# Two batches rounded together in the last feed-forward layer, and layer 1 attention's output product moved into the next batch's first gap

## Chip, cores and metric

One NeuronCore of a Trainium2 chip runs the whole kernel. The metric is the device time of one execution in microseconds (us), the median of three. PE is TensorE (its matrix engine), PEld its weight loads, DVE is VectorE, ACT is ScalarE, POOL is GpSimd, SP is SyncE, which issues the DMAs. Matmul results land in eight PSUM banks, called `banks` in the profile; all else lies in SBUF, in one large tensor called `memory`.

## What is computed

A four-layer decoder on x of shape 8 batches x 112 rows x 256 columns, float32; each layer is attention, cross attention and a feed-forward part, each behind a layer norm and added to x. Two of the twelve parts matter here.

Layer 1 attention (16 heads of 16), with a fixed near-diagonal matrix L mixed into the attention:

```
A_stable = LAMBDA_JUMP * A + (1.0 - LAMBDA_JUMP) * L[None, None, :, :]
out = jnp.einsum('bhqk,bhkd->bhqd', A_stable, V)
out = out.transpose(0, 2, 1, 3).reshape(B, S, D)
return out @ Wo.T + bo
```

The last part, layer 3's feed-forward, rounds the inputs of all three matmuls to four-bit values with a scale for each block of 16:

```
amax = jnp.max(jnp.abs(xb), axis=-1, keepdims=True)
sc = jnp.clip(amax / FP4_MAX * global_scale, 0.0, FP8_MAX)
sc8 = sc.astype(jnp.float8_e4m3fn).astype(jnp.float32)
dq = sc8 / global_scale
a = jnp.clip(jnp.abs(xb) / safe_dq, 0.0, FP4_MAX)
q = jnp.sign(xb) * _FP4_VALS[jnp.digitize(a, _FP4_MIDS)]
...
gate_out = nvfp4_linear(x, gate_w, s_in[0])
up_out = nvfp4_linear(x, up_w, s_in[0])
hidden = jax.nn.silu(gate_out) * up_out
return nvfp4_linear(hidden, down_w, s_in_down[0])
```

The hidden rows are 8 x 112 x 1024.

## The kernel before

The twelve parts run one after the other, with a barrier of all engines between them. Within a part every engine has its own program, written by walking one generator, `order()`, which yields steps such as ("turn", 3); each engine emits what it has to do for a step and skips the others. Nothing reorders afterwards: an engine works its own list strictly in this order and waits on semaphores (`wait_ge`) for the others. So `order()` sets what stands behind what on each engine.

**Layer 3's feed-forward, class `L3Ffn`.** It quantizes ten units of 112 x 1024: units 0 and 1 are the normalized input rows ("rows", four batches side by side), units 2 to 9 the hidden rows of batches 0 to 7. For a unit, DVE takes each block's largest magnitude (`tensor_reduce`), works out the scales in nine small instructions on 64 columns (`four_bit_scales`), scales the unit (`tensor_tensor`), clamps it and cuts out each value's power of two (two `tensor_scalar`), multiplies that to a rounding constant (a third `tensor_scalar`), and adds and subtracts the constant (two `tensor_tensor`): that rounds. GpSimd multiplies by the block scales and writes bf16 (`four_bit_values`). PE transposes the unit (step "turn"), ACT copies it out of PSUM; for hidden units PE then multiplies by the down weights and DVE adds the result to x (step "sum"). Step "gate" is the gate and up matmuls of a batch (PE), the Silu (ACT), and their product into `hids` (DVE, the "hid" instruction). In `order()` a hidden unit b is rounded ("four", b + 2), then comes gate b + 1, then the sum of b - 1, then the turn of b.

**Layer 1 attention, class `L1Attn`** on `TiledSelf`. For batch b: the scores of all 16 heads ("all", PE), their maxima (four `tensor_reduce` on DVE), 16 exponentials (ACT, "weights"), four groups of transposes ("turned"), a transposed table of 1/sum ("inverse"), the products with V ("products"), their scaling on DVE ("norm", into `oT`) and the addition of the near-diagonal part on GpSimd, then the output product ("y", PE). The projections k, q, v, the near-diagonal product and the norm of coming batches fill gaps between these; the tuple `plan` says which step of which batch (0, +1, +2) stands in which of five gaps: after turned 0, 1, 2, behind turned 3 and the exponentials, and at the batch's end. PSUM banks for y, k, q, near, v, xT, inverse and products are handed out in turn from a ring of two (6 and 7) by `next_bank`; `fill` makes PE wait until the bank's last content has been read. So whichever step stands two places further back in PE's list must have been read before a step may start.

## Time and profile before

| what | value |
|---|---|
| median of 3 runs | 2310.19 us (2309.71 to 2314.41) |
| the profiled execution's own time | 2309.87 us |
| its span | 2308.1 us |
| busy PE / DVE / ACT / POOL over the span | 88% / 59% / 39% / 24% |
| TensorE clock granted, mean | 0.865 of full speed |
| layer 1 attention in the trace | 640.29 to 748.83 us |
| layer 3's feed-forward in the trace | 2185.85 to 2303.25 us |

In a timeline row stand: start in us, length in us, engine, line, operation, out<-in with partitions x elements, how many were merged (x8), and in brackets how long the engine sat idle before it and who ended that. In a windows row stand: stretch, its length, then busy us (and count of instructions) of PE, PEld, DVE, ACT and POOL, then the granted TensorE clock (1.00 is 2.4 GHz, half of it 1.2 GHz), the DMA share and GB/s. In a group row stand: count | busy us, mean ns of one | idle before. Consecutive instructions of one engine that do not depend on each other overlap by about 0.1 us at their ends.

### The profile page before, as it was taken

The page shows a single profiled execution, that of the slowest core. Times are in us where ns is not written, and L with a number is a line of the kernel's source. Part 1 is how long each engine was busy: PE and PEld are TensorE (multiplying, and loading weights), DVE is VectorE, ACT ScalarE, POOL GpSimd, SP SyncE. Part 2 cuts the span into 40 slices and gives each one's busy share as a digit, 9 for nine tenths or more (in the row PEclk, how much of TensorE's full clock was granted, in tenths as well). Part 3 has the DMA queues.
Part 4 walks back from the last instruction along what each step waited for, and adds up shares of the span by engine and source line. Part 5 has one row for each costly group of instructions (what it writes and reads, how often), then busy time and mean ns, then how long its engine had stood idle before and what let it go on. Part 6 is the DMA issues. An engine that isn't in the chain of part 4 may idle for free.

```text
span 2308.1 us, 57670 instructions
## 1 busy us (share of the span) xinstructions
PE 2019.8 (88%) x22720; PEld 1471.6 (64%) x22720; DVE 1353.8 (59%) x3602; ACT 896.5 (39%) x3421; POOL 561.4 (24%) x1358
## 2 busy tenths in 40 slices
PE   8999999989977898998977887999999999789744
PEld 4899998877566565567855654666554545556522
DVE  6667666755255787545635624787263220678797
ACT  2455554543155564212334422665110111256511
POOL 3566664222011000102425512331000000401111
PEclk9555555999989899899988988999999999889956
DMA  3000002004000001100030000000030000000000
GB/s 136 4 5 5 5 5 79 1 1 182 0 5 2 14 12 53 86 0 24 1 133 2 1 1 7 9 11 2 1 151 0 1 0 4 1 15 12 2 0 16
DMA packets 8027, 57.21 MB, mean 25 GB/s; under 512 B 793, under 2 KB 5249, under 8 KB 5985
## 3 DMA queue, kind: packets, MB, share of 16 engines
q1 hardware_dynamic: 7760, 53.54, 6.1%
q8 instruction: 183, 3.00, 0.5%
q14 instruction: 84, 0.68, 0.1%
HBM read 52.62 MB, written 0.92 MB: 23 GB/s over the span
## 4 chain that ended last, share of the span: by engine, by line
PE 67%; DVE 12%; issue 9%; ACT 6%; POOL 5%; DMA 1%; POOLq 0%; DVEq 0%; SPq 0%; ACTq 0%
PE banks L265 43%; PE banks L270 8%; PE banks L1364 7%; PE banks L937 3%; ACT memory L985 2%; PE banks L963 2%; DVE memory L1466 2%; PE banks L1517 1%; DVE memory L1247 1%; ACT memory L1391 1%; DVE memory L824 1%; POOL memory L1423 1%; ACT memory L1398 1%; DVE memory L1472 1%; DVE memory L1475 1%
## 5 line engine op out<-in xcount | busy, mean ns | idle before, releaser
L265 PE MATMUL banks<-memory 128*112 128x256 f32 (+7 forms) x4192 | 1129.8, 425 | 65.9 <-POOL memory L2077 8.0
L265 PEld LDWEIGHTS banks<-memory 128*128 128x128 f32 (+3 forms) x4192 | 704.8, 195 | 396.4 <-issue 250.9
L270 PE MATMUL banks<-memory 112*125 112x112 f32 (+3 forms) x2000 | 305.9, 286 | 108.6 <-DVE memory L824 54.9
L270 PEld LDWEIGHTS banks<-memory 112*125 112x125 f32 (+3 forms) x2000 | 238.6, 172 | 224.6 <-issue 114.6
L1364 PE MATMUL banks<-memory 128*128 128x8 bf16 (+2 forms) x10752 | 308.1, 174 | 13.7 <-DVE memory L1449 1.4
L1364 PEld LDWEIGHTS banks<-memory 128*128 128x128 bf16 x10752 | 296.7, 104 | 25.7 <-POOL memory L1423 21.5
L985 ACT ACTIVATE memory<-banks,memory 112x375 f32<-112x375 f32 x384 | 215.4, 579 | 25.5 <-DVE memory L1023 25.1
L1023 DVE TENSOR_REDUCE memory<-banks 112x2 f32<-112x750 f32 x192 | 171.1, 934 | 37.1 <-PE banks L937 36.9
L1466 DVE TENSOR_REDUCE memory<-banks 128x48 f32<-128x192 f32 x448 | 122.1, 291 | 62.6 <-PE banks L1364 47.9
L840 POOL TENSOR_TENSOR memory<-memory 112x1 f32<-112x1 f32 x71 | 39.2, 552 | 355.7 <-DVE memory L819 354.3
L1031 DVE COPY memory<-banks 125x448 f32<-125x448 f32 x192 | 117.0, 620 | 10.5 <-PE banks L270 6.1
L1545 ACT ACTIVATE memory<-memory 112x112 f32<-112x112 f32 x192 | 71.7, 375 | 87.8 <-DVE memory L1566 87.8
L937 PE MATMUL banks<-memory 32*112 32x375 f32 x768 | 88.5, 529 | 19.5 <-ACT memory L985 17.3
L1007 ACT COPY memory<-banks 125x448 f32<-125x448 f32 x96 | 51.2, 533 | 127.8 <-PE banks L270 127.8
L3213 DVE TENSOR_TENSOR memory<-banks,memory 112x256 f32<-112x256 f32 x8 | 3.4, 425 | 157.6 <-PE banks L265 157.6
L1391 ACT ACTIVATE memory<-memory 128x48 f32<-128x48 f32 x224 | 54.4, 243 | 97.5 <-DVE memory L1466 97.4
L1405 ACT COPY banks<-memory 128x48 f32<-128x48 f32 x448 | 80.1, 179 | 23.8 <-DVE memory L1445 23.8
L1230 ACT ACTIVATE memory<-banks,memory 112x112 f32<-112x112 f32 x256 | 86.4, 391 | 6.7 <-DVE memory L1247 5.3
L3187 ACT ACTIVATE memory<-banks,memory 128x448 f32<-128x448 f32 x32 | 20.3, 635 | 173.5 <-PE banks L265 173.5
L985 ACT ACTIVATION_READ_ACCUMULATOR memory<-banks,memory 112x1 f32 x384 | 80.5, 210 | 0.0
L963 PE MATMUL banks<-memory 125*32 125x112 f32 x2304 | 76.2, 265 | 1.4 <-DVE memory L1031 1.4
L1423 POOL TENSOR_TENSOR memory<-memory 128x16 f32<-128x16 f32 x224 | 49.9, 223 | 102.2 <-ACT memory L1398 102.1
(234 smaller groups left out, 2425.2 us busy)
## 6 DMA issues: line engine op xcount, KB each, us to landing
memory<-in_l2x SPq DMA_DIRECT2D x1, 7680.0 KB, 21.6
memory<-in_l2f SPq DMA_DIRECT2D x1, 7168.0 KB, 20.1
memory<-in_l1f SPq DMA_DIRECT2D x1, 4617.0 KB, 14.8
memory<-in_ctxT SPq DMA_DIRECT2D x24, 187.5 KB
memory<-in_l2f SPq DMA_DIRECT2D x1, 4096.0 KB, 12.6
memory<-in_l3f SPq DMA_DIRECT2D x1, 3073.0 KB, 22.4
memory<-in_l2a SPq DMA_DIRECT2D x1, 3072.0 KB, 18.2
memory<-in_l0f SPq DMA_DIRECT2D x1, 2304.0 KB, 9.1
```

Of the source, the lines that this page charges most:

```text
L265: ins = self.nc.tensor.matmul(out, weights[i], acts[i], start=i == 0, stop=i == n - 1)
L270: return self.nc.tensor.transpose(out, in_, self.ident[0:n, 0:n])
L937: ins = PE.matmul(k.bank(bank, S, CK), q, kT, start=True, stop=True)
L963: ins = PE.matmul(k.banks[32 * r:32 * r + 32, 6, t * S:(t + 1) * S], v, PT_sb[0:CR, c, r * S:(r + 1) * S], start=c == 0 and m == 0, stop=c ...
L985: self.nc.scalar.activation(self.P_both[gi % 2][:, r, :], self.k.bank(r, S, CK), ACT.Exp, bias=u["nmax"][:, 4 * i + r:4 * i + r + 1], scal ...
L1023: V.tensor_reduce(u["nmax"][:, 4 * i + 2 * h:4 * i + 2 * h + 2], k.banks[0:S, 2 * h:2 * h + 2, 0:CK], AX, ALU.max, negate=True).then_inc(* ...
L1031: V.tensor_copy(self.PT_both[gi % 2][0:CR, c, :], k.bank(k.at["turn", gi, c], CR, 4 * S)).then_inc(*s.pt_v.up())
L1230: A.activation(self.P_all[:, i, g, :], k.bank(i, S, 4 * S)[:, g * S:(g + 1) * S], ACT.Exp, bias=u["nmax"][:, 4 * i + g:4 * i + g + 1], sca ...
L1364: ins = self.nc.tensor.matmul(own[:, part:3, at:at + B], self.whh[:, part, l, j, g * P:(g + 1) * P], self.upper[l][:, 0:3 - part, j * B:(j ...
L1391: A.activation(self.gates[:, l, 1:4, :].rearrange("p g c -> p (g c)"), self.sums[:, l, 0:6 * B], ACT.Tanh).then_inc(*s.act_tanh.up())
L1405: self.nc.scalar.copy(self.slots[l][last][:, 3, :], src).then_inc(*self.s.xw_in.up())
L1466: V.tensor_reduce(self.sums[:, l, first * B:end * B], self.slots[l][last].rearrange("p s c -> p c s"), AX, ALU.add).then_inc(*s.gates_in.up())
```

## The change

In layer 1 attention y of batch b moves from gap 4 of batch b to gap 0 of batch b + 1 (the last one behind the loop), stats moves two gaps earlier, xn one gap earlier, and v from gap 2 into gap 3, where xT joins it. In layer 3's feed-forward hidden units are rounded two at a time: the small scale instructions work on 128 columns and the scaling on 2048; the constant's multiplication goes from DVE to ACT as `Relu(ROUND * t - ROUND)`, and the two `tensor_tensor` become two `scalar_tensor_tensor` that put ROUND back. GpSimd starts both products of a pair when the second difference is done; the last two units' products go to DVE. The transposes alternate between two banks, `hT` has two buffers, and the walk of `order()` is written anew.

```diff
 class L1Attn(TiledSelf):
...
-    plan = ((("k", 0, 1),), (("q", 0, 1), ("near", 0, 0)), (("v", 0, 1), ("stats", 0, 2)), (("xn", 0, 2),),
-            (("xT", 0, 2), ("y", 0, 0)))
-    tail = ()
+    plan = ((("y", 0, -1), ("k", 0, 1), ("stats", 0, 2)), (("q", 0, 1), ("near", 0, 0)), (("xn", 0, 2),),
+            (("v", 0, 1), ("xT", 0, 2)), ())
+    tail = (("y", 0),)
...
+ROUND = 1.5 * 2.0 ** 22
...
 class L3Ffn:
...
     def order(self):
         yield "norm", B - 1
-        yield "four", 0
-        yield "four", 1
+        yield "rows", 0
+        yield "powers", 0
+        yield "round", 0
         yield "turn", 0
+        yield "rows", 1
+        yield "powers", 1
         yield "gate", 0
-        yield "turn", 1
-        for b in range(B):
-            yield "four", b + 2
-            if b + 1 < B:
-                yield "gate", b + 1
-            if b:
-                yield "sum", b - 1
+        yield "hid", 0
+        yield "gate", 1
+        yield "round", 1
+        yield "top", 0
+        yield "hid", 1
+        yield "top", 1
+        for p in range(HALF):
+            last = p == HALF - 1
+            yield "scale", p
+            if not last:
+                yield "gate", 2 * p + 2
+                yield "hid", 2 * p + 2
+            if p:
+                yield "turn", 2 * p
+            yield "powers", 2 * p + 2
+            yield "powers", 2 * p + 3
+            if not last:
+                yield "gate", 2 * p + 3
+            yield "turn", 2 * p + 1
+            sums = [("sum", b) for b in (2 * p - 2, 2 * p - 1) if p]
+            if last:
+                yield from sums
+            yield "round", 2 * p + 2
+            yield "round", 2 * p + 3
+            if not last:
+                yield "hid", 2 * p + 3
+                yield "top", 2 * p + 2
+                yield "top", 2 * p + 3
+                yield from sums
+        for b in (B - 2, B - 1):
             yield "turn", b + 2
-        yield "sum", B - 1
+        for b in (B - 2, B - 1):
+            yield "sum", b
...
+    def dve_round(self, n):
+        k, s, V = self.k, self.s, self.nc.vector
+        y, t = self.half(self.y, n), self.half(self.t, n)
+        V.wait_ge(*s.step_ready(n + 1))
+        V.scalar_tensor_tensor(out=y, in0=t, scalar=ROUND, in1=y, op0=ALU.add, op1=ALU.add).then_inc(*s.vstep.up())
+        V.wait_ge(*s.vstep.now())
+        V.scalar_tensor_tensor(out=y, in0=t, scalar=ROUND, in1=y, op0=ALU.add,
+                               op1=ALU.subtract).then_inc(*s.sums_ready.up())
+        if n >= self.LAST - 1:
+            V.wait_ge(*s.sums_ready(n + 1))
+            V.wait_ge(*s.tp16_full(n - 1))
+            four_bit_values(V, self.values[n % 2], y, self.scales(n)[:, 1]).then_inc(*s.last_ready.up())
...
     def pool(self):
+        norm_row(k, B - 1, k.stats, s.stat_ready(1), s.rstd_ready).then_inc(*s.xn_ready.up())
+        for n in range(self.LAST - 1):
+            G.wait_ge(*s.sums_ready(n + 1 if n < 2 else (n | 1) + 1))
+            if n >= 2:
+                G.wait_ge(*s.tp16_full(n - 1))
+            four_bit_values(G, self.values[n % 2], self.half(self.y, n), self.scales(n)[:, 1]).then_inc(*s.quant_ready.up())
...
     def act(self):
         k, s, A = self.k, self.s, self.nc.scalar
+        A.wait_ge(*s.wq_ready(1))
+        A.activation(self.sg[:, 0:1], self.minus, ACT.Silu)
         for step, i in self.order():
-            if step == "gate":
+            if step == "powers":
+                t = self.half(self.t, i)
+                A.wait_ge(*s.pow_ready(i + 1))
+                A.activation(t, t, ACT.Relu, bias=self.minus, scale=ROUND).then_inc(*s.step_ready.up())
+            elif step == "gate":
```

Lines of shared helpers lie three further down in the changed kernel. These rows stand in DVE's list of the last part before, from one unit's reciprocal to the next unit's maxima (L3429 is the hid instruction, L3448 the sum):

```order
L2812 RECIPROCAL memory<-memory 112x64
L2800 TENSOR_SCALAR memory<-memory 112x64
L2794 TENSOR_TENSOR memory<-memory 112x1024
L2800 TENSOR_SCALAR memory<-memory 112x1024
L2798 TENSOR_SCALAR memory<-memory 112x1024
L2800 TENSOR_SCALAR memory<-memory 112x1024
L2794 TENSOR_TENSOR memory<-memory 112x1024
L3445 TENSOR_TENSOR memory<-memory 112x1024
L3429 SCALAR_TENSOR_TENSOR memory<-banks,memory 112x1024
L3448 SCALAR_TENSOR_TENSOR memory<-banks,memory 112x256
L3257 TENSOR_REDUCE memory<-memory 112x64
```

And these in the changed kernel, from one pair's reciprocal on (L3496 is the hid instruction, L3523 and L3525 the two of `dve_round`):

```order
L2815 RECIPROCAL memory<-memory 112x128
L2803 TENSOR_SCALAR memory<-memory 112x128
L2797 TENSOR_TENSOR memory<-memory 112x2048
L3496 SCALAR_TENSOR_TENSOR memory<-banks,memory 112x1024
L2803 TENSOR_SCALAR memory<-memory 112x1024
L2801 TENSOR_SCALAR memory<-memory 112x1024
L2803 TENSOR_SCALAR memory<-memory 112x1024
L2801 TENSOR_SCALAR memory<-memory 112x1024
L3523 SCALAR_TENSOR_TENSOR memory<-memory 112x1024
L3525 SCALAR_TENSOR_TENSOR memory<-memory 112x1024
L3523 SCALAR_TENSOR_TENSOR memory<-memory 112x1024
L3525 SCALAR_TENSOR_TENSOR memory<-memory 112x1024
```

Between scaling and difference, one unit's three `tensor_scalar` have become two units' two each; the two adds are of the fused form and stand in a block of four.

On ACT the last rows of the program before are these (L3505 is the Silu, L3516 the copy of a transposed hidden unit):

```order
L3505 ACTIVATE memory<-banks,memory 112x1024
L3516 COPY memory<-banks 128x896
L3505 ACTIVATE memory<-banks,memory 112x1024
L3516 COPY memory<-banks 128x896 x2
```

In the changed kernel they are these (L3585 is the Relu, L3590 the Silu, L3601 the copy):

```order
L3585 ACTIVATE memory<-memory 112x1024 x2
L3590 ACTIVATE memory<-banks,memory 112x1024
L3601 COPY memory<-banks 128x896 x2
L3585 ACTIVATE memory<-memory 112x1024 x2
L3601 COPY memory<-banks 128x896 x3
```

The last two Relus, of units 8 and 9, stand behind the copies of units 5 and 6 and ahead of those of units 7, 8 and 9.

In PE's list of layer 1 attention, with the semaphores that a row waits for, this stood before from turned 3 of a batch to turned 0 of the next (L265 with 112x256 is y, L1214 the products, L270 with 128x112 first the inverse and then xT):

```order
L270 MATMUL banks<-memory 112x112 [waits pt_a,exp_done]
L270 MATMUL banks<-memory 112x112 x3
L270 MATMUL banks<-memory 128x112 [waits near_ready,inv_ready]
L270 MATMUL banks<-memory 128x112
L1214 MATMUL banks<-memory 32x112 [waits pt_v,pt_a,v_ready]
L1214 MATMUL banks<-memory 32x112 x15
L270 MATMUL banks<-memory 128x112 [waits r_ready,xn_ready]
L270 MATMUL banks<-memory 128x112
L265 MATMUL banks<-memory 112x256 [waits o_ready,oT_ready]
L265 MATMUL banks<-memory 112x256
L270 MATMUL banks<-memory 112x112 [waits pt_a,exp_done]
```

And this stands there now, from behind turned 3 to y (the first L268 is v, the second y; L273 with 128x112 is first xT and then the inverse):

```order
L268 MATMUL banks<-memory 112x256 [waits q_ready,xT_ready]
L268 MATMUL banks<-memory 112x256
L273 MATMUL banks<-memory 128x112 [waits near_ready,xn_ready]
L273 MATMUL banks<-memory 128x112
L273 MATMUL banks<-memory 128x112 [waits v_ready,inv_ready]
L273 MATMUL banks<-memory 128x112
L1217 MATMUL banks<-memory 32x112 [waits pt_v,pt_a,xT_ready,v_ready]
L1217 MATMUL banks<-memory 32x112 x15
L273 MATMUL banks<-memory 112x112 [waits pt_a,exp_done]
L273 MATMUL banks<-memory 112x112 x3
L268 MATMUL banks<-memory 112x256 [waits r_ready,oT_ready]
L268 MATMUL banks<-memory 112x256
```

The inverse now waits for v_ready, because its bank held v, and the products for xT_ready.

## Rows read from the trace of the kernel before

**Rows 1.** Windows: six batches of layer 1 attention, one of them, the last part.

```profile
663.74:740.07 76.33, 61.62 (x694) 51.80 (x694) 41.99 (x120) 47.06 (x226) 8.84 (x17) 0.89 0.01 2
716.13:727.68 11.55, 9.04 (x117) 7.52 (x117) 7.21 (x21) 7.93 (x39) 1.56 (x3) 1.00 0.01 1
2185.85:2303.25 117.40, 49.50 (x208) 32.10 (x208) 106.50 (x181) 19.26 (x19) 21.11 (x12) 0.60 0.00 0
```

**Rows 2.** Timeline of DVE, one hidden unit of the last part.

```profile
2241.88 1.21 DVE L3257 TENSOR_REDUCE memory<-memory 112x64 f32<-112x1024 f32 x1
2243.12 0.25 DVE L2800 TENSOR_SCALAR memory<-memory 112x64 f32<-112x64 f32 x1
...
2245.73 1.23 DVE L2794 TENSOR_TENSOR memory<-memory 112x1024 f32<-112x1024 f32 x1
2246.99 0.69 DVE L2800 TENSOR_SCALAR memory<-memory 112x1024 f32<-112x1024 f32 x1
...
2249.18 1.23 DVE L2794 TENSOR_TENSOR memory<-memory 112x1024 f32<-112x1024 f32 x1
...
2251.58 1.28 DVE L3429 SCALAR_TENSOR_TENSOR memory<-banks,memory 112x1024 f32<-112x1024 f32 x1
...
2253.16 1.21 DVE L3257 TENSOR_REDUCE memory<-memory 112x64 f32<-112x1024 f32 x1
```

**Rows 3.** Timeline of DVE, a 128-column scale chain in the weights' quantization.

```profile
1715.13 0.29 DVE L2800 TENSOR_SCALAR memory<-memory 128x128 f32<-128x128 f32 x1
...
1718.47 2.29 DVE L2794 TENSOR_TENSOR memory<-memory 128x2048 f32<-128x2048 f32 x1
```

**Rows 4.** Groups by line and shape, of DVE and of ACT.

```profile
L2803 DVE SCALAR_TENSOR_TENSOR memory<-memory 112x256 f32<-112x256 f32 x1 | 0.4, 424 | 0.0
L1376 ACT ACTIVATE memory<-memory 128x1024 f32<-128x1024 f32 x2 | 2.1, 1050 | 0.0
```

**Rows 5.** Timeline of all engines, the first products and gates of the last part.

```profile
2196.81 1.93 POOL L3248 TENSOR_TENSOR memory<-memory 112x1024 bf16<-112x1024 f32 x1 [7.95 <-DVE memory L3445]
2197.89 0.90 DVE L2800 TENSOR_SCALAR memory<-memory 112x64 f32<-112x64 f32 x1
...
2204.65 1.11 ACT L3505 ACTIVATE memory<-banks,memory 112x1024 f32<-112x1024 f32 x1 [2.45 <-PE banks L265]
...
2206.99 1.28 DVE L3429 SCALAR_TENSOR_TENSOR memory<-banks,memory 112x1024 f32<-112x1024 f32 x1
...
2209.86 3.23 PE L265 MATMUL banks<-memory 128*112 128x512 bf16 x8
```

**Rows 6.** Timeline of all engines, the end of the last part.

```profile
2298.86 0.93 PE L3494 MATMUL banks<-memory 112*128 112x112 bf16 x8 [7.44 <-POOL memory L3248]
2299.82 0.91 ACT L3516 COPY memory<-banks 128x896 bf16<-128x896 bf16 x1 [10.41 <-PE banks L3494]
...
2302.77 0.48 DVE L3448 SCALAR_TENSOR_TENSOR memory<-banks,memory 112x256 f32<-112x256 f32 x1 [5.59 <-PE banks L265]
```

**Rows 7.** Timelines of PE and DVE in layer 1 attention: y, all, v's bias, maxima, last products.

```profile
716.13 1.12 PE L265 MATMUL banks<-memory 128*112 128x256 f32 x4 [0.82 <-POOL memory L2077]
717.08 0.55 PE L270 MATMUL banks<-memory 112*112 112x112 f32 x4
...
720.92 1.03 PE L265 MATMUL banks<-memory 128*112 128x256 f32 x4
...
735.08 1.05 PE L1190 MATMUL banks<-memory 32*112 32x112 f32 x32
...
735.19 0.49 DVE L1109 TENSOR_TENSOR memory<-banks,memory 112x128 f32<-112x128 f32 x2 [1.33 <-PE banks L265]
...
736.20 2.22 DVE L1247 TENSOR_REDUCE memory<-banks 112x4 f32<-112x448 f32 x4 [0.15 <-PE banks L1190]
...
744.51 0.98 PE L1214 MATMUL banks<-memory 112*32 112x112 f32 x32 [0.46 <-ACT memory L1238]
746.80 1.12 PE L265 MATMUL banks<-memory 128*112 128x256 f32 x4 [1.30 <-POOL memory L2077]
```

More of the change, by code:

```diff
@@ L3258, in four_bit_scales, with four_bit_steps @@
                     apply_absolute_value=True).then_inc(*s.vstep.up())
+def four_bit_scales(k, src, gs, sc, sign=1.0):
+    four_bit_tops(k, src, sc[:, 0])
+    four_bit_steps(k, gs, sc, sign)
+def four_bit_steps(k, gs, sc, sign=1.0):
+    c = Chain(k)
+    top, s8, c8 = sc[:, 0], sc[:, 1], sc[:, 2]
     c.ts(top, top, 1.0 / 6.0, gs, ALU.mult, ALU.mult)
@@ L3373 @@
     UNITS = (("rows", 0), ("rows", 1)) + tuple(("hidden", b) for b in range(B))
+    LAST = B + 1
     def __init__(self, k):
@@ L3380, in __init__ @@
         self.ident16 = take(P, dt=BF16)
-        self.y, self.t = [take(HID, parts=S) for _ in range(2)], take(HID, parts=S)
-        self.sc = [take(3, HID // 16, parts=S) for _ in range(2)]
+        two = lambda *dims, dt=F32: [take(*dims, dt=dt, parts=S) for _ in range(2)]
+        self.hids, self.y, self.t = two(2 * HID), two(2 * HID), two(2 * HID)
+        self.sc = two(3, 2 * HID // 16)
         self.xT = four_bit_rows(k)
-        self.values = [take(HID, dt=BF16, parts=S) for _ in range(2)]
@@ L3385, in __init__ @@
-        self.sg, self.hids = take(HID, parts=S), take(2, HID, parts=S)
-        self.hT = take(8, S, dt=BF16)
+        self.values = two(HID, dt=BF16)
+        self.sg = take(HID, parts=S)
+        self.hT = [take(8, S, dt=BF16) for _ in range(2)]
+        self.minus = take(1, parts=S)
     def order(self):
         yield "norm", B - 1
-        yield "four", 0
-        yield "four", 1
+        yield "rows", 0
+        yield "powers", 0
+        yield "round", 0
         yield "turn", 0
+        yield "rows", 1
@@ L3412, in run, with half, scales @@
+        for b in (B - 2, B - 1):
+            yield "turn", b + 2
+        for b in (B - 2, B - 1):
+            yield "sum", b
+    def half(self, a, n):
+        pair = a[(n // 2 + 1) % 2]
+        return pair[:, n % 2 * self.HID:(n % 2 + 1) * self.HID]
+    def scales(self, n):
+        return self.sc[(n // 2 + 1) % 2][:, :, n % 2 * self.HID // 16:(n % 2 + 1) * self.HID // 16]
     def run(self):
@@ L3421, in dve @@
     def dve(self):
-        k, s, V, st = self.k, self.s, self.nc.vector, self.k.stats
+        k, s, V, st, w = self.k, self.s, self.nc.vector, self.k.stats, self.w
+        V.memset(self.minus, -ROUND)
         V.tensor_copy(self.ident16, k.ident).then_inc(*s.wq_ready.up())
@@ L3426, in dve @@
                 norm_row_stats(k, i, st, s.stat_ready)
-            elif step == "gate":
+            elif step == "rows":
+                if i:
+                    V.wait_ge(*s.xn_ready(1))
+                src = k.row_norms[:, i * HALF:(i + 1) * HALF, :].rearrange("p b d -> p (b d)")
+                y = self.half(self.y, i)
+                four_bit_scales(k, src, w["s_in"][0:S, 0:1], self.scales(i), -1.0)
+                four_bit_scaled(k, src, y, self.scales(i))
+            elif step == "hid":
+                hid = self.half(self.hids, i + 2)
@@ L3428, in dve @@
                 V.wait_ge(*s.silu_ready(i + 1))
                 V.scalar_tensor_tensor(
-                    out=self.hids[:, i % 2, :].rearrange("p (h n) -> p h n", h=2), in0=k.banks[0:S, 2:4, :],
-                    scalar=self.inv[0:S, 1:2], in1=self.sg.rearrange("p (h n) -> p h n", h=2), op0=ALU.mult,
+                    out=hid.rearrange("p (h n) -> p h n", h=2), in0=k.banks[0:S, 2:4, :], scalar=self.inv[0:S, 1:2],
+                    in1=self.sg.rearrange("p (h n) -> p h n", h=2), op0=ALU.mult,
@@ L3432, in dve @@
                     op1=ALU.mult).then_inc(*s.hid_ready.up())
-            elif step == "four":
-                kind, b = self.UNITS[i]
-                if kind == "hidden":
-                    V.wait_ge(*s.hid_ready(b + 1))
-                elif b:
-                    V.wait_ge(*s.xn_ready(1))
-                if i >= 2:
-                    V.wait_ge(*s.quant_ready(i - 1))
-                src, gs = self.rows_of(i)
-                four_bit_scales(k, src, gs, self.sc[i % 2])
-                four_bit_sums(k, src, self.y[i % 2], self.t, self.sc[i % 2])
-                V.wait_ge(*s.vstep.now())
-                V.tensor_tensor(self.y[i % 2], self.y[i % 2], self.t, ALU.subtract).then_inc(*s.sums_ready.up())
+            elif step == "top":
+                V.wait_ge(*s.hid_ready(i + 1))
+                four_bit_tops(k, self.half(self.hids, i + 2), self.scales(i + 2)[:, 0])
+            elif step == "scale":
+                sc = self.sc[i % 2]
+                if i:
+                    V.wait_ge(*s.quant_ready(2 * i))
+                four_bit_steps(k, w["s_in"][0:S, 1:2], sc, -1.0)
+                four_bit_scaled(k, self.hids[i % 2], self.y[i % 2], sc)
+            elif step == "powers":
+                four_bit_powers(k, self.half(self.y, i), self.half(self.t, i), s.pow_ready)
+            elif step == "round":
+                self.dve_round(i)
```

66 lines of the change are left out of this document (29 added, 37 removed).

## The prediction

> **What bounds the kernel now.** I read the windows first, then each engine's timeline inside the two parts that the change touches, since a mean over the span mixes stages with different limits.
>
> In the last part DVE is busy 106.50 of 117.40 us, PE 49.50, ACT 19.26 and GpSimd 21.11 [rows 1]. Its list is the path: one hidden unit takes from one maxima instruction to the next 2253.16 - 2241.88 = 11.28 us, and none of the rows between shows an idle bracket [rows 2]. What the reader is to see there: the scale chain of nine small instructions takes 2245.73 - 2243.12 = 2.61, the scaling 1.26, each of the three passes over 1024 columns 2.19 / 3 = 0.73, add and subtract together 2.40, the hid instruction with the sum behind it 1.58, the maxima 1.24. PE, ACT and GpSimd only matter at the part's two ends.
>
> In layer 1 attention PE is the path. A batch takes 11.55 us at a granted clock of 1.00, with 9.04 us of PE work in it; the six batches from 663.74 on take 76.33 at 0.89 [rows 1]. So 76.33 - 6 x 11.55 = 7.0 us there go with the lower of the two clocks. PE's idle 11.55 - 9.04 = 2.5 us of a batch lie behind turned 3, in three pieces: ahead of the inverse, ahead of xT, and 0.82 ahead of y, which GpSimd's addition ends [rows 7].
>
> **Layer 3's feed-forward, step by step.** Every time below counts from the start of GpSimd's first product, 2196.81 before [rows 5]; the part ended 2303.25 - 2196.81 = 106.44 later [rows 1].
>
> *Ahead of it.* Unit 0's third pass (0.73 less the 0.04 gap) becomes a Relu on ACT. The nearest row is an ACT activation of 1024 columns from SBUF, 1.05 us [rows 4]; with some 0.05 each way it is 1.15. DVE has nothing else there: +0.5.
>
> *Opening.* Unit 1's maxima end at 1.04, its first scale instruction sits out GpSimd's product as it did before (0.90 instead of 0.25 [rows 2, 5]), and its powers end at 1.08 + 2.61 + 0.65 + 1.26 + 1.42 = 7.0. Its Relu stands ahead of Silu 0 on ACT and ends at 8.1, Silu 0 (1.11) at 9.3, so hid 0 starts at 9.3; before it started at 10.2, behind unit 1's rounding [rows 5]. Gate 1 needs hid 0's banks: 10.6 + 3.2 to 3.7 for the matmuls [rows 5], Silu 1 until 15.1. DVE meanwhile does round 1 and one maxima (2.4 + 1.2, to 14.2), waits 0.9, then hid 1 (1.3) and maxima (1.25): the first pair's scale chain starts at 17.7.
>
> *A pair.* The 128-column chain takes 1718.47 - 1715.13 = 3.34 [rows 3], against 2 x 2.61. The 2048-column scaling is 2.29 [rows 3], 2.22 to the next start. Two clamps and two powers 2.8, four fused instructions 4.82, two hids 2.4, two maxima 2.4, two sums 0.8: 18.75, against 22.56. The fused price is from DVE: 0.424 us for 256 columns with SBUF sources [rows 4], plus 768 columns at the slope of the same form with a PSUM source, (1.28 - 0.48) / 768 = 1.04 ns [rows 2, 6], gives 1.22, what a `tensor_tensor` costs (1.23 [rows 2]). A pair saves 1.9 in the chain, 1.5 by the passes that moved, 0.2 in the scaling and the rest in overlapped ends. The Relus hide: Relu n starts while DVE does the powers of n + 1, 1.4 against 1.15. If that cover were gone a pair would pay 0.3. GpSimd's two products take 3.9 behind the second difference; hid, two maxima and two sums cover 4.4. In the first pair no sums stand there, 3.7 of cover, and the first scale instruction waits 0.3. Three pairs: (18.75 - 0.8 + 0.1 + 0.3) + 2 x 18.75 = 55.9, so 73.6.
>
> *Last pair.* Chain and scaling 5.7, powers 2.8: 8.5. Then the sums of batches 4 and 5 stand ahead of the rounding. Sum 5 needs the down product of unit 7, and in ACT's list that unit's copy stands behind both Relus of units 8 and 9. Relu 9 ends at 9.6; copy to down product to sum takes 2302.77 - 2299.82 = 2.95 [rows 6]; sum 5 starts at 12.5, 3.7 late, with the rounding queued behind it. Then 0.4, two roundings (2.5 each) and two products, now DVE's (1.15 and 1.23): 20.3, so 93.9. From the last product to the end: transposes at 0.1, then 2303.25 - 2298.86 = 4.4 [rows 1, 6]: 98.4.
>
> *Sum.* 98.4 + 0.5 = 98.9 against 106.4: **7.5 us saved**. Bounds: 11.2 if the 3.7 us stall is not there; 5 if hand-overs cost half a us more in each pair and at the opening.
>
> **Layer 1 attention, step by step.** I count from the start of a batch's "all". The maxima start 736.20 - 735.08 = 1.12 later when DVE is free [rows 7], and it is: stats and v's bias have left their place ahead of them. They take 2.12 to the next start, v's bias addition 0.49 [rows 7]: done at 3.73. The inverse's bank held v, so PE waits for it although its input is long ready: start 3.9, products 4.2. In the last batch before, where DVE had nothing else, the way from the products' start to y's was 746.80 - 744.51 = 2.29 [rows 7], so y could start at 6.5. PE has turned 0 of the next batch meanwhile (0.39, a 0.55 row less its tail), so 0.8 us of idle stay ahead of y. From y to v it was 720.92 - 716.13 = 4.79 [rows 7]; less turned 0 that is 4.40 from y to the next "all". Period 6.51 + 4.40 = **10.91 against 11.55**: 0.63 x 6 = 3.8. The cover for y comes, but the waits ahead of inverse and xT become one wait for v's bias through the bank. At the start v leaves the way to the first counted "all" (+0.96, v's pitch); in the last two batches ACT's exponentials bound as before, and y of batch 6 now stands between them: -0.6. **4.1 us saved** at unchanged clock losses.
>
> What hides nothing here: xn and its copy move with slack of 1 us; GpSimd's power step for stats now comes early and holds up nobody. No DMA is moved.
>
> **The clock** is the unknown: 7.0 us at the lower level now. The stretch with gaps stays about as sparse (1.7 us of work between turned 3 and y in 4.2 before; 2.0 in 4.0 after), so I leave the loss as it is. Bounds: all of it given back (another 7), or as much as 4 more lost.
>
> Together 7.5 + 4.1 = 11.6 off the profiled execution's own 2309.87, whose median is 2310.19: **2298.3**.
>
> **Rivals.**
> 1. *The clock stays up in layer 1 attention.* For it: the longest idle piece is no longer threefold. Against: the idle sum falls only from 2.5 to 1.9 a batch. 2298.3 - 7 = 2291.
> 2. *Layer 1 gives nothing*: the bank order costs what the cover gives, or the clock falls in more batches. For it: v_ready and xT_ready in PE's waits. 2298.3 + 4.1 = 2302.4.
> 3. *The last part's stall is not there or the hand-overs are dearer*: 2294.6 to 2301.
> 4. *The fused instruction runs at half rate*, and the change loses. Twenty of them lie on DVE's path; at one column in 2.08 ns each costs 1.07 more: 21.4, so 2298.3 + 21.4 = 2319.7. It turns into a loss from 11.6 / 20 = 0.58 us more each. Against it is the 0.424 us row, which at half rate would be near 0.69 [rows 4]; for it, that it is a single small instance. The Trainium skill, "Vector Engine (DVE) Microarchitecture Reference", section 7 "Points that are easy to get wrong", says that `S2S2D2_STT` with two non-bf16 SBUF sources halves throughput. By that rule the time would be rival 4's; this trace's row disagrees with it.
> 5. *The change does not do what it says in the last part* (ACT switching tables between Relu and Silu, 1.28 us each, say): the build has one table load there, so I leave it out.
>
> **Chances.** Forecast with the small variations of rival 3: 0.66. Clock regained: 0.14. Layer 1 nothing: 0.15. Half rate or an unseen stall of that size: 0.05. The range has to leave out no more than 2 in 10: 2291.5 takes in most of rival 1, 2303.5 rival 2. Within 0.2% (4.6 us; about what a measurement of this kernel can tell) of 2310.19 would need both parts to disappoint. Faster 0.94, same 0.025, slower 0.035.
>
> **What the changed profile would show.** Last part 110 us long instead of 117.4, pairs of 18.8; fused instructions at 1.22; one DVE idle bracket near 3.7 ahead of the sum in the last pair, ended by PE, and about 2.3 and 0.9 ahead of hids 0 and 1; the first scale instruction behind each product block not stretched but once. In layer 1 a period of 10.9 at clock 1.00, PE idle 1.1 ahead of the inverse ended by DVE's v bias, 0.8 ahead of y ended by GpSimd. Wrong would be: fused instructions above 1.3, periods of 11.5 at full clock, or a mean clock in that part off 0.89.

## The result and the profile after

The changed kernel takes 2288.38 us (median of 4 runs, 2288.00 to 2296.15) against 2310.01; the ratio is 0.991 with a 95% interval of 0.9886 to 0.9934. Two more series of it gave 2290.31 and 2290.49 against 2310.48 and 2310.74 (0.9913 and 0.9912). The forecast was 2298.3 with a range of 2291.5 to 2303.5: the right direction, and a gain of 20 to 22 us where 11.6 was forecast.

The windows that answer to [rows 1], of the kernel after. The first is the stretch from VectorE's first reading of y to its seventh, then two batches of it (at full clock, and with a fall of the clock), then the last part from its begin and from GpSimd's first product:

```profile
666.42:734.44 68.02, 55.87 (x696) 47.47 (x695) 42.46 (x120) 46.96 (x228) 9.08 (x17) 0.96 0.01 2
666.42:677.39 10.97, 8.94 (x118) 7.64 (x117) 7.31 (x22) 7.83 (x38) 1.60 (x3) 1.00 0.01 1
688.36:700.18 11.82, 9.78 (x118) 8.17 (x117) 7.31 (x22) 7.83 (x38) 1.61 (x3) 0.92 0.01 2
2174.50:2283.00 108.50, 48.47 (x208) 30.36 (x208) 93.17 (x129) 29.39 (x30) 17.12 (x10) 0.59 0.00 1
2185.00:2281.92 96.92, 48.47 (x208) 30.36 (x208) 84.33 (x113) 27.36 (x27) 15.33 (x8) 0.61 0.00 0
```

The same stretch, y to y, in the kernel before:

```profile
665.83:741.23 75.40, 60.68 (x697) 51.23 (x696) 41.98 (x121) 46.27 (x221) 8.84 (x17) 0.91 0.01 2
```

What the reader is to see: the full-clock batch has the length that was worked out (10.97, forecast 10.91), but the six together save 75.40 - 68.02 = 7.4 us and not 6 x 0.63 = 3.8. PE's own busy time fell from 60.68 to 55.87 with the same matmuls: they ran longer at the higher clock.

PE's timeline in a batch after, answering to [rows 7]:

```profile
682.99 0.36 PE L273 MATMUL banks<-memory 112*128 112x112 f32 x2
684.59 0.38 PE L273 MATMUL banks<-memory 112*128 112x112 f32 x2 [1.24 <-DVE memory L1112]
684.91 0.98 PE L1217 MATMUL banks<-memory 112*32 112x112 f32 x32
685.82 0.59 PE L273 MATMUL banks<-memory 112*112 112x112 f32 x4
687.21 2.00 PE L268 MATMUL banks<-memory 128*112 128x256 f32 x12 [0.80 <-POOL memory L2080]
```

Two waits are left, the ones forecast: ahead of the inverse for v's bias (1.24, forecast 1.1), and ahead of y for GpSimd (0.80, forecast 0.8).

DVE's timeline in the last part: the first fused instructions, hid 0, hid 1, the first scale instruction of each pair, and the sum of batch 5 with its round behind it:

```profile
2182.43 1.23 DVE L3523 SCALAR_TENSOR_TENSOR memory<-memory 112x1024 f32<-112x1024 f32 x1 [1.21 <-ACT memory L3585]
2183.70 1.22 DVE L3525 SCALAR_TENSOR_TENSOR memory<-memory 112x1024 f32<-112x1024 f32 x1
...
2194.23 1.28 DVE L3496 SCALAR_TENSOR_TENSOR memory<-banks,memory 112x1024 f32<-112x1024 f32 x1 [2.22 <-ACT memory L3590]
...
2199.41 1.28 DVE L3496 SCALAR_TENSOR_TENSOR memory<-banks,memory 112x1024 f32<-112x1024 f32 x1 [0.38 <-ACT memory L3590]
...
2201.99 0.29 DVE L2803 TENSOR_SCALAR memory<-memory 112x128 f32<-112x128 f32 x1
...
2220.01 0.29 DVE L2803 TENSOR_SCALAR memory<-memory 112x128 f32<-112x128 f32 x1
...
2238.62 0.28 DVE L2803 TENSOR_SCALAR memory<-memory 112x128 f32<-112x128 f32 x1
...
2257.22 0.28 DVE L2803 TENSOR_SCALAR memory<-memory 112x128 f32<-112x128 f32 x1
...
2269.64 0.48 DVE L3515 SCALAR_TENSOR_TENSOR memory<-banks,memory 112x256 f32<-112x256 f32 x1 [3.62 <-PE banks L268]
2270.04 1.22 DVE L3523 SCALAR_TENSOR_TENSOR memory<-memory 112x1024 f32<-112x1024 f32 x1
```

The fused instruction costs 1.22 us, as forecast. The pairs take 18.02, 18.61 and 18.60. The one large wait, 3.62, stands where it was said to stand.

### The profile page after: what moved, and what is told of

Read it like the earlier page. It is cut to its first block, busy times and chain, and to the rows that moved or that the text cites. A ratio compares the mean times of both kernels' runs of the same rounds, so it can differ in the third digit from the quotient of the medians.

```text
span 2286.7 us, 57634 instructions
## 1 busy us (share of the span) xinstructions
PE 2009.9 (88%) x22720; PEld 1463.9 (64%) x22720; DVE 1341.2 (59%) x3555; ACT 906.6 (40%) x3432; POOL 559.5 (24%) x1356
## 4 chain that ended last, share of the span: by engine, by line
PE 68%; DVE 15%; ACT 6%; issue 6%; POOL 4%; DMA 1%; POOLq 0%; DVEq 0%; SPq 0%; ACTq 0%
PE banks L268 44%; PE banks L273 8%; PE banks L1367 6%; PE banks L940 3%; ACT memory L988 2%; PE banks L966 2%; DVE memory L1469 2%; PE banks L1520 1%; ACT memory L1394 1%; POOL memory L1426 1%; ACT memory L1401 1%; DVE memory L1250 1%; DVE memory L827 1%; DVE memory L1475 1%; DVE memory L1478 1%
## 5 line engine op out<-in xcount | busy, mean ns | idle before, releaser
L268 PE MATMUL banks<-memory 128*112 128x256 f32 (+8 forms) x4192 | 1126.8, 424 | 95.5 <-DVE memory L3496 21.9
L268 PEld LDWEIGHTS banks<-memory 128*128 128x128 f32 (+3 forms) x4192 | 699.5, 194 | 428.9 <-issue 275.7
L273 PE MATMUL banks<-memory 112*125 112x112 f32 (+3 forms) x2000 | 301.6, 283 | 104.5 <-DVE memory L827 53.2
L273 PEld LDWEIGHTS banks<-memory 112*125 112x125 f32 (+3 forms) x2000 | 235.6, 170 | 219.7 <-issue 123.9
L1426 POOL TENSOR_TENSOR memory<-memory 128x16 f32<-128x16 f32 x224 | 49.8, 222 | 100.8 <-ACT memory L1401 100.7
## 6 DMA issues: line engine op xcount, KB each, us to landing
memory<-in_l1f SPq DMA_DIRECT2D x1, 4617.0 KB, 16.7
```

The source lines that it names most:

```text
L268: ins = self.nc.tensor.matmul(out, weights[i], acts[i], start=i == 0, stop=i == n - 1)
L273: return self.nc.tensor.transpose(out, in_, self.ident[0:n, 0:n])
```

## The experiments

The clock of one and the same program differs from trace to trace. So I read the effect of an edit from the length of the edited part, and the time beside it. "Stretch" is the first to the seventh y of layer 1 attention (75.4 before), "last part" runs from GpSimd's first product to VectorE's end (106.4 before, 96.9 after).

**Each half alone.** `e1` keeps the old `L3Ffn`; `e2` takes the old order in `L1Attn`. The edit of e2 (e1's is its reverse, on the kernel before):

```diff
-    plan = ((("y", 0, -1), ("k", 0, 1), ("stats", 0, 2)), (("q", 0, 1), ("near", 0, 0)), (("xn", 0, 2),),
-            (("v", 0, 1), ("xT", 0, 2)), ())
-    tail = (("y", 0),)
+    plan = ((("k", 0, 1),), (("q", 0, 1), ("near", 0, 0)), (("v", 0, 1), ("stats", 0, 2)), (("xn", 0, 2),),
+            (("xT", 0, 2), ("y", 0, 0)))
+    tail = ()
```

> The kernel before with the new order of layer 1 attention alone; layer 3's feed-forward is the old one. If the traces of before and after add up part by part (8.7 us less in layer 1 attention, 5.7 less in the unchanged parts between it and 1400 us, 9.0 in the last part), the time is about 2297 to 2299 and the six batches' stretch shows a granted clock near 0.97 instead of 0.89. Rival: the gain outside the two edited parts needs both edits, or is chance; then only the 4.1 us that I worked out for the order itself are there, 2306.

> The change without the new order of layer 1 attention: layer 3's feed-forward alone. By the traces 9.0 us less than before, 2301; by the sum of the prediction 7.5 less, 2302.7. Rival: the last part's gain depends on the clock phase that the earlier parts leave, so that it comes out under 7 or above 11. The batches of layer 1 attention are to take 11.55 us at full clock and their stretch about 76 us at 0.89, as before.

Before, in this series, 2308.62 us. e1: 2299.45, ratio 0.9958 (0.9943 to 0.9973), stretch 68.0, last part 106.4. e2: 2300.96, 0.9966 (0.9953 to 0.9979), stretch 75.4, last part 96.8. Each half brings its own part's saving and leaves the other part as it was. The two savings, 9.2 and 7.7 us, add up to 16.9.

**Later start.** Does the clock depend on when the batches begin? At the begin of layer 1 attention, in the kernel before (e3) and after (e4):

```diff
         self.nc.vector.wait_ge(*self.k.landed["l1a"].now())
...
+        V.memset(self.y_sb, 0.0).then_inc(*self.s.vstep.up())
+        for _ in range(5):
+            c.ts(self.y_sb, self.y_sb, 0.0, None, ALU.mult)
...
```

> The kernel before, and VectorE does some 2.5 us of idle work (a memset and five multiplications of 112x256) when layer 1 attention begins: the same batches, started later. Theory one (the order of a batch decides how often the clock falls): the stretch of six batches stays at 75 to 77 us and 0.88 to 0.90, and the whole takes 2310 to 2313. Theory two (the moment at which the batches meet the clock's own timing decides): the stretch moves by 2 us or more in either direction, its clock with it.

> The changed kernel with the same 2.5 us of idle work at the start of layer 1 attention. Theory one: the stretch of six batches stays near 67 us at 0.97, the whole 2288 to 2292. Theory two: the clock falls more often again, the stretch is 69 to 74 us at 0.90 to 0.95, and some of the 5.7 us of the parts behind it go too; 2293 to 2300.

e3: 2309.87, ratio 1.0003, stretch 75.1. e4: 2293.28, 0.9939 (0.9922 to 0.9957), stretch 68.9. In e3 the first y is read 2.6 us later than before (668.43 against 665.83), and the stretch stays as it was: theory one. e4 tests less. Its first y comes only 0.4 us later than in the first trace of the changed kernel (666.86 against 666.42), because unedited parts ahead of it were shorter. Its time missed the 2288 to 2292 of theory one and falls into the range of theory two. Its stretch of 68.9 is one that the unedited changed kernel has too, as its second trace below shows. But e3's trace shows something else. From VectorE's last reading of y to the same scaling instruction in layer 3's weights, nobody edited anything. Its two rows in e3:

```profile
750.26 0.42 DVE L808 TENSOR_TENSOR memory<-banks,memory 112x256 f32<-112x256 f32 x1 [2.01 <-PE banks L265]
...
1717.25 2.29 DVE L2800 TENSOR_TENSOR memory<-memory 128x2048 f32<-128x2048 f32 x1
```

That is 966.99 us. In the kernel before it is 1718.47 - 747.95 = 970.5, from [rows 3] and this row:

```profile
747.95 0.42 DVE L808 TENSOR_TENSOR memory<-banks,memory 112x256 f32<-112x256 f32 x1 [2.01 <-PE banks L265]
```

So e3 has 3.5 us less there, for no reason in the program.

**The change once more**, unedited, and a third time:

> The changed kernel once more, unedited, on this chip and in more rounds. If what came out beyond the 9.5 us of the last part and the 8.0 to 8.7 us of layer 1 attention (another 3 to 4 us, in parts that nobody edited) belongs to the change, the median is 2287 to 2289. If it is chance of the clock in unchanged parts, the median is nearer to 2290 to 2293, single runs spread over 6 us or more, and the trace puts part of the difference elsewhere than the first one did.

> The changed kernel, unedited, for a comparison on one chip with the next. 2288 to 2291 us, stretch of layer 1 attention 68 to 69 us, last part 97 or 98 us.

2290.31 us (2289.25 to 2293.64) and 2290.49 (2289.07 to 2291.84). The same two rows of the changed kernel, in the first trace:

```profile
741.42 0.42 DVE L811 TENSOR_TENSOR memory<-banks,memory 112x256 f32<-112x256 f32 x1 [2.01 <-PE banks L268]
...
1706.14 2.29 DVE L2797 TENSOR_TENSOR memory<-memory 128x2048 f32<-128x2048 f32 x1
```

and in the second:

```profile
739.47 0.42 DVE L811 TENSOR_TENSOR memory<-banks,memory 112x256 f32<-112x256 f32 x1 [2.01 <-PE banks L268]
...
1710.28 2.29 DVE L2797 TENSOR_TENSOR memory<-memory 128x2048 f32<-128x2048 f32 x1
```

964.7 us and 970.8: one program, 6.1 us apart. So a single trace's gain behind layer 1 attention can be chance. The begin of layer 1 attention, VectorE's first copy, also lies at another time in each trace, though the parts ahead of it are unedited. Before and after (first trace):

```profile
640.84 0.39 DVE L827 COPY memory<-banks 128x224 f32<-128x224 f32 x1 [0.65 <-PE banks L270]
```

```profile
642.94 0.39 DVE L830 COPY memory<-banks 128x224 f32<-128x224 f32 x1 [0.65 <-PE banks L273]
```

All differences to the profiled execution before, in us, from such rows:

| stretch | first | second | third |
|---|---|---|---|
| up to layer 1 attention's first copy (unedited) | +2.1 | -1.3 | +1.9 |
| from there to the first y | -1.5 | -0.2 | -1.6 |
| six batches, first to seventh y | -7.4 | -6.5 | -7.4 |
| last y | +0.3 | -0.5 | +0.2 |
| last y to layer 3's scaling (unedited) | -5.8 | +0.3 | -5.8 |
| to GpSimd's first product (0.5 of it edited) | +0.5 | +0.4 | +3.1 |
| last part | -9.5 | -8.5 | -8.5 |
| sum | -21.3 | -16.3 | -18.1 |

The edited parts, with the 0.5 us of the Relu ahead of the last one, give 17.6, 15.2 and 16.7 us in the three traces. The medians of the three series lie 21.6, 20.2 and 20.2 us under their kernel before, so 4.0, 5.0 and 3.6 us more. In e2 it is the other way: 7.7 us by the median, about 9.1 by its trace. Whether the change has a share in these 4 to 5 us is open: no run tests it.

The last part has two lengths, 96.9 and 98.0. They part at gate 1's matmuls, in the first and the second trace, where the granted clock is 0.71 and 0.50:

```profile
2195.66 2.57 PE L268 MATMUL banks<-memory 128*112 128x512 bf16 x8 [2.91 <-DVE memory L3496]
```

```profile
2199.72 3.63 PE L268 MATMUL banks<-memory 128*112 128x512 bf16 x8 [2.91 <-DVE memory L3496]
```

**Which step of layer 1's order counts.** e5 moves y alone, e6 moves v, stats, xn and xT alone (both on the kernel before):

```diff
+    plan = ((("y", 0, -1), ("k", 0, 1)), (("q", 0, 1), ("near", 0, 0)), (("v", 0, 1), ("stats", 0, 2)), (("xn", 0, 2),),
+            (("xT", 0, 2),))
+    tail = (("y", 0),)
```

```diff
+    plan = ((("k", 0, 1), ("stats", 0, 2)), (("q", 0, 1), ("near", 0, 0)), (("xn", 0, 2),), (("v", 0, 1), ("xT", 0, 2)),
+            (("y", 0, 0),))
```

> Before, with only y moved behind the next batch's scores; v, stats and xT keep their places. Theory one (what keeps the clock up is that the wait ahead of y, at the end of three waits in a row, has gone): a batch takes 10.7 to 11.1 us at full clock, the stretch from the first y to the seventh 66 to 69 us instead of 75.4, the time 2299 to 2302. Theory two (it takes both, the other order of v and stats as well): the clock falls in most batches as before, the stretch is 71 to 74 us, the time 2304 to 2306.

> Before, with v and stats in their new places and y still at the end of its own batch. By the prediction's sum this pays for the wait for v's bias and gets no cover for y: 11.5 to 11.9 us a batch at full clock. Theory one: the stretch stays at 74 to 78 us and the time at 2308 to 2312. Theory two: the clock falls less often, 70 to 73 us, 2304 to 2306.

A full-clock batch and the stretch, of e5 and then of e6:

```profile
666.07:677.32 11.25, 9.12 (x118) 7.65 (x118) 7.29 (x22) 7.12 (x35) 1.55 (x3) 1.00 0.01 1
666.07:734.55 68.48, 56.88 (x697) 47.34 (x697) 42.47 (x120) 45.94 (x221) 8.82 (x17) 0.95 0.01 2
```

```profile
677.52:688.89 11.37, 8.81 (x118) 7.60 (x117) 7.20 (x21) 7.81 (x38) 1.60 (x3) 1.00 0.01 2
664.11:737.75 73.64, 58.38 (x696) 50.40 (x695) 41.84 (x121) 46.96 (x228) 9.04 (x17) 0.92 0.01 2
```

y alone gives 6.9 of the stretch's 7.4, the rest alone 1.8. In e5 the clock stays up although PE still waits three times in a full-clock batch:

```profile
672.73 0.41 PE L270 MATMUL banks<-memory 112*128 112x112 f32 x2 [0.79 <-POOL memory L1063]
674.96 0.77 PE L270 MATMUL banks<-memory 112*128 112x112 f32 x6 [0.91 <-DVE memory L1259]
676.16 1.55 PE L265 MATMUL banks<-memory 128*112 128x256 f32 x8 [0.44 <-POOL memory L2077]
```

The times, 2303.47 and 2304.31 (0.997 and 0.9973), don't tell the two apart. e5's is 1.5 us over theory one's range, while its stretch lies in it; its period is 11.15 to 11.25, over the 10.7 to 11.1 forecast. e6's stretch fits neither theory (73.6, just under the one and over the other), and its median lies 4.4 us under what the stretch gives; its trace has 6 us less in the unedited parts behind. The stretch answers the question of the order, not the whole difference of the times.

**What brings the clock down.** The changed kernel with 1, 3 and 6 idle multiplications on VectorE ahead of v's bias, so that PE waits longer for the inverse. The run with three:

```diff
+    def dve_value(self, u, i, rows, bk):
...
+        for _ in range(3):
+            V.wait_ge(*s.vstep.now())
+            V.tensor_scalar(self.pad, self.pad, 0.0, None, ALU.mult).then_inc(*s.vstep.up())
+        super().dve_value(u, i, rows, bk)
```

> The changed kernel with one multiplication of 112x256 on VectorE (0.42 us) ahead of v's bias in every batch of layer 1 attention, so that TensorE waits that much longer ahead of the inverse. Full-clock period 10.97 + 0.42 = 11.39 us. If the clock falls by how long TensorE idles in a batch, the old loss of 5 to 6 us comes back: the stretch from the first y to the seventh is 73 to 75 us. If it goes by where the waits lie (one wait ahead of y less), the loss stays at 2 to 3 us: 68.5 + 6 x 0.42 = 71 us.

> As the run with one added multiplication a batch, but three of them, one behind the other: by that run each lengthens the full-clock period by 0.20 us, so 11.58 here, and TensorE idles 2.6 us a batch, a little more than in the kernel before (2.5). If the length of the idle sum brings the clock down, the stretch from the first y to the seventh is 6 x 11.58 + 5.5 = 75 us. If it matters that the waits lie elsewhere, the loss stays at 2 to 3 us: 72 us.

> Six added multiplications a batch, full-clock period 12.2 us, TensorE idle 3.2 us a batch. By the idle sum the loss to the clock is 6 us or more, the stretch 79 us or longer. By the place of the waits it is still 2 to 3 us, 76 us.

2293.96, 2303.46 and 2321.62 us, the last two in one run each. A batch and the stretch, of one, three and six:

```profile
674.89:686.07 11.18, 8.95 (x118) 7.64 (x117) 7.51 (x22) 7.81 (x38) 1.60 (x3) 1.00 0.01 2
663.72:733.44 69.72, 56.38 (x697) 48.06 (x696) 43.67 (x127) 46.80 (x228) 9.05 (x17) 0.95 0.01 2
```

```profile
681.09:694.44 13.35, 10.46 (x118) 8.86 (x118) 8.10 (x25) 7.83 (x38) 1.60 (x3) 0.88 0.01 2
666.16:747.69 81.53, 65.33 (x696) 55.15 (x696) 47.22 (x139) 47.19 (x228) 9.07 (x17) 0.83 0.01 2
```

```profile
673.04:687.02 13.98, 10.48 (x118) 8.74 (x118) 8.98 (x27) 7.83 (x38) 1.60 (x3) 0.87 0.01 1
673.04:764.80 91.76, 70.36 (x696) 59.17 (x696) 52.52 (x156) 47.29 (x228) 9.07 (x17) 0.78 0.01 1
```

PE's idle time of a batch is its length less its busy time. It is given for the batch shown (before: the one of [rows 1]), and as the mean of the six of the stretch; with three and six added no batch is at full clock. What the clock costs in the stretch is PE's busy time less six times that of a full-clock batch (for the padded runs the changed kernel's 8.94). In order of the first:

| kernel | idle a batch | mean of six | lost to the clock in six |
|---|---|---|---|
| after | 2.03 | 2.03 | 2.2 |
| y alone | 2.13 | 1.93 | 2.2 |
| after, one added | 2.23 | 2.22 | 2.7 |
| before | 2.51 | 2.45 | 6.4 |
| v and the rest alone | 2.56 | 2.54 | 5.5 |
| after, three added | 2.89 | 2.70 | 11.7 |
| after, six added | 3.50 | 3.57 | 16.7 |

How far one program varies, the changed order's second trace shows, and the version of both ends below, which has the same order in this part:

```profile
664.34:733.26 68.92, 56.81 (x697) 48.78 (x697) 42.40 (x120) 46.70 (x228) 9.05 (x17) 0.95 0.01 2
```

```profile
663.22:730.23 67.01, 54.88 (x697) 46.86 (x696) 42.45 (x121) 46.60 (x228) 9.05 (x17) 0.97 0.01 2
```

They lose 3.2 and 1.2 us, at the same idle sum. So differences of 1 to 2 us in the last column say nothing, and with it the one pair that is out of order. What is left is clear of that: 1.2 to 3.2 us at 2.0 to 2.2 of idle, 5.5 and 6.4 at 2.5, 11.7 and 16.7 beyond. A straight line between one and three added gives 6.5 us at the 2.51 of the kernel before, whose waits lie elsewhere; it lost 6.4.

I had favoured the place of the waits after the run with one; the runs with three and six refute it as the only cause. That it has a smaller share beside the sum is not excluded: no run moves the waits at an equal sum. My numbers for these two were off by a lot (75 and 79 us against 81.5 and 91.8): a multiplication added 0.25 to 0.29 us, not 0.20, and I had taken the loss to level off at 5.5 or 6. The longest single wait is no better a guide: with one added it is 1.44 us, against 0.8 to 0.9 in a full-clock batch of the kernel before, at less than half its loss.

**Products early.** GpSimd's product as soon as its unit is rounded:

```diff
-            G.wait_ge(*s.sums_ready(n + 1 if n < 2 else (n | 1) + 1))
+            G.wait_ge(*s.sums_ready(n + 1))
```

> The changed kernel, where GpSimd starts a unit's product as soon as that unit's rounding is done, beside VectorE's rounding of the pair's second unit, instead of behind both. Read by the last part's length in the trace (96.9 us now). If the product and VectorE's work disturb each other wherever they meet, as the scale instruction of 0.90 instead of 0.25 us suggests, a pair loses 0.65 us or more: 98.9 to 101. Rival: only that small instruction is touched and the fused ones run through, 96.3 to 97.2.

Last part 101.6, 4.7 us longer (2296.37 us in one run). The pair's rows of DVE and POOL:

```profile
2235.26 1.23 DVE L3525 SCALAR_TENSOR_TENSOR memory<-memory 112x1024 f32<-112x1024 f32 x1
2236.41 1.22 DVE L3523 SCALAR_TENSOR_TENSOR memory<-memory 112x1024 f32<-112x1024 f32 x1
2236.57 2.85 POOL L3254 TENSOR_TENSOR memory<-memory 112x1024 bf16<-112x1024 f32 x1 [13.69 <-DVE memory L3525]
2237.66 2.83 DVE L3525 SCALAR_TENSOR_TENSOR memory<-memory 112x1024 f32<-112x1024 f32 x1
2240.42 1.27 DVE L3496 SCALAR_TENSOR_TENSOR memory<-banks,memory 112x1024 f32<-112x1024 f32 x1
2240.57 1.93 POOL L3254 TENSOR_TENSOR memory<-memory 112x1024 bf16<-112x1024 f32 x1 [1.16 <-DVE memory L3525]
2241.61 2.52 DVE L3261 TENSOR_REDUCE memory<-memory 112x64 f32<-112x1024 f32 x2
```

The last fused instruction takes 2.83 instead of 1.23 us, and the product 2.85 instead of 1.93. The rows read as if the two took turns: the product begins while the fused instruction at 2236.41 runs, which keeps its 1.22 us; the product ends 1.79 us behind that one (2239.42 less 2237.63), and the next fused instruction ends 1.07 us behind the product. Hid (one input in PSUM) and the maxima (one input) run beside the second product at their usual lengths. All three pairs show the same, and lose 1.6 each. The scale instruction of [rows 5], a `tensor_scalar` with one input in SBUF, is held up too: it ends at 2198.79, the product beside it at 2198.74. The Trainium skill, "GPSIMD Engine Reference", section 2 "Architecture", says that GpSimd's SBUF read and write port are shared with VectorE; the trace agrees for the instruction that reads two SBUF inputs, and shows no cost for hid and the maxima.

**Third pass back on VectorE**, in place of the Relu:

```diff
-                four_bit_powers(k, self.half(self.y, i), self.half(self.t, i), s.pow_ready)
+                c = four_bit_powers(k, self.half(self.y, i), self.half(self.t, i))
+                c.ts(self.half(self.t, i), self.half(self.t, i), 1.0, ROUND, ALU.max, ALU.mult)
...
```

> The changed kernel with the third pass back on VectorE (0.69 us a unit, then a plain addition and subtraction); no Relu on ScalarE. By the ledger: hid 0 starts 0.3 us earlier, three pairs take 1.4 more each, the last pair 1.4 more and its wait of 3.62 is gone: 96.9 - 0.3 + 4.2 + 1.4 - 3.6 = 98.6 us for the last part. Rival: the wait is not the Relus' doing and stays, 102.2; or the Relus' hand-overs cost VectorE something hidden, and it comes out under 97.5.

Last part 100.7, 2295.06 us in one run. 1.0 of the 2.1 us over the forecast is the slower gate 1 seen above; each pair pays 1.7 instead of 1.4. The wait ahead of sum 5 is gone, as the ledger said. Handing the pass to ScalarE is worth 100.7 - 98.0 = 2.7 us at the same slow gate 1, the stall that it brings already paid.

**The last pair's stall taken away.** e7 puts unit 7's transposes and copy ahead of the last two Relus; e11 also puts gate 0's Silu ahead of unit 1's Relu. The edit of both, and the second one of e11:

```diff
+            if last:
+                yield "turn", 2 * p + 1
             yield "powers", 2 * p + 2
             yield "powers", 2 * p + 3
             if not last:
                 yield "gate", 2 * p + 3
-            yield "turn", 2 * p + 1
+                yield "turn", 2 * p + 1
```

```diff
         yield "rows", 1
+        yield "gate", 0
         yield "powers", 1
-        yield "gate", 0
         yield "hid", 0
```

> The changed kernel, where in the last pair alone the transposes and the copy of unit 7 stand ahead of ScalarE's two Relus. If sum 5 was late only because that copy stood behind both Relus, VectorE's wait of 3.62 us is gone and the last part takes 96.9 - 3.6 = 93.3 us, up to 93.8 if the copy makes the first Relu late; the time is 3.3 us below the changed kernel's of the same chip. Rival: something else ends last there (GpSimd's products of units 6 and 7, the down product behind them) and under 1.5 us are saved.

> The changed kernel with unit 7's transposes and copy ahead of the last pair's Relus, and gate 0's Silu ahead of unit 1's Relu. The first gave 93.1 us for the last part where the profile of the same program phase had 96.9 to 98.0; the second moves hid 0 forward by 0.3 us: 92.8 us, and a time 3.5 to 4.5 us under the changed kernel's, 2284.5 to 2287. Rival: Relu 1 now ends later and round 1 waits, so that the opening gains nothing: 93.1 to 93.6.

> The version with unit 7's copy ahead of the last pair's Relus and gate 0's Silu ahead of unit 1's Relu, once more. By the traces 4.5 us under the changed kernel: 2284 to 2286, last part 92.5 or 93.5 us. If the earlier 2284.7 was luck of the clock in unedited parts, 2286 to 2288.

e7: last part 93.1, 2289.17 us (0.9905, 0.989 to 0.992). Both sums and the round behind them:

```profile
2269.33 0.69 DVE L2801 TENSOR_SCALAR memory<-memory 112x1024 int32<-112x1024 int32 x1
2269.94 0.87 DVE L3517 SCALAR_TENSOR_TENSOR memory<-banks,memory 112x256 f32<-112x256 f32 x2
...
2270.73 1.22 DVE L3525 SCALAR_TENSOR_TENSOR memory<-memory 112x1024 f32<-112x1024 f32 x1
```

No bracket is left; from the last powers to the round it is 1.4 us instead of 5.1. The time of that series hardly shows it: 1.1 us under the changed kernel's, where 3.3 were forecast. e11: last part 92.4 in both traces, 0.4 us under the forecast, because gate 1, with its clock at 1.00, took 1.91 us. 2284.73 us (0.989, 0.9874 to 0.9907), and again 2285.39 (0.9893, 0.9876 to 0.9909) beside the changed kernel's 2290.49 on the same chip. It is the fastest version, by 5.1 us there; the last part is 4.5 to 5.5 us shorter than in the traces of the changed kernel. The intervals of the two ratios still overlap, so the part's length is the stronger evidence.

## Why the prediction was wrong, step by step

**The step that failed** is "The stretch with gaps stays about as sparse ..., so I leave the loss as it is". The waits were sized rightly, so the idle sum of a batch fell from 2.5 to 2.0 us, and with it the clock's toll went from 6.4 to 2.2 us (3.2 in the second trace). Rival 1 is what happened, in part: 3 to 4 of its 7 us came back, and it had 0.14. Its argument against itself, "the idle sum falls only from 2.5 to 1.9", was the very quantity that counts. The measured gain of the stretch, 6.5 to 7.4, is the forecast 3.8 (3.5 as measured, 6 x 0.58) and 3 to 4 of clock. The Trainium skill, "TensorE: Matmul & The Clock Gate", section "A second HAM failure mode: psum-queue depth-cycling", describes a clock that swings because TensorE idles in small pieces between groups; this trace agrees, with no wait above 1.24 us and a granted clock of 0.91 to 0.93 in three of six batches.

**The last part was mis-sized** by 1.5 us (96.9 against 98.4); the time came out shorter than the sum. The opening took 17.0 and not 17.7: gate 1's matmuls needed 2.57 us where I had taken 3.2 to 3.7 from [rows 5], so hid 1 waited 0.38 and not 0.9. With gate 1 wholly at the lower clock (3.63 us) the part is 98.0, near the forecast. The three pairs took 55.2, not 55.9: the first meets no GpSimd wait, for which the sum had 0.3, and the other two are 0.15 short each. The Relus are hidden, the fused price is exact, sum 5's stall of 3.7 is 3.62 with the cause that was named (e7). Ahead of the part the Relu cost 0.5 as said: DVE waited 1.21 for it in place of a 0.73 pass.

**Rival 4**, half rate for the fused instruction, is refuted by all its instances: 1.22 to 1.23 us for 1024 columns, like a `tensor_tensor`. The rule that the prediction cites from the Trainium skill, "Vector Engine (DVE) Microarchitecture Reference", section 7 "Points that are easy to get wrong", does not hold in this trace.

**What the prediction lacked** is the noise of unedited parts. One and the same program took 964.7 or 970.8 us between two of its instructions; single runs lie up to 8 us apart. The range of 12 us held only my edits' unknowns. What decides a run's clock in those parts stays open: e3 and e4, with idle work put ahead, have 967.0 and 964.4, within the spread of the rest.

**Taken together**: the first profile gained 21.3 us, 9.7 more than forecast. 4.5 of these are layer 1 attention, from its first copy to its last y (8.6 against 4.1: the six periods gave 3.5 where 3.8 were forecast, the clock 3.9 where nothing was, the start 1.5 and not 0.96, the end cost 0.3 and not 0.6). 1.5 are the last part (9.5 less the 0.5 ahead of it, against 7.5), and 3.7 fell in unedited parts, where the second trace shows 1.0 and the third 1.3. With the edited parts' 17.6 us alone the time would be near 2292.4, inside the stated range. What put the median out of it, to 2288.38, and the other two just out of it, is the 4 to 5 us whose origin is open.

## What to carry to other kernels

Where TensorE's granted clock is below 1.00 in a stretch, price a change there by what it does to TensorE's idle sum and not only by the waits: at 2 to 3 us of idle in an 11 us batch, 0.5 us less idle gave back another 0.5 to 0.7 us of clock, and 0.9 more cost 1.6. Put GpSimd's elementwise work beside VectorE's maxima or an instruction with an input in PSUM, not beside one with two SBUF inputs; a `tensor_scalar` with one SBUF input was held up too (0.90 instead of 0.25 us). Judge an edit by its part's length in two or three traces before reading a difference of a few microseconds in the total.
